# Two chained attention blocks on one core: the transpose that closes each pass of row maxima is put two jobs later

## The reference: what is computed

```
x = x + block0(groupnorm(x))    # per image: 1024 queries x 1024 keys, scores*0.25 + rel_h + rel_w, softmax, @v, projection
x = x + block1(groupnorm(x))    # per image: 7x7 neighbourhood + 16 register keys, mask, softmax, @v, projection
```

## The kernel before

| row job | stage | step | its phase starts at |
|---|---|---|---|
| L0 phase 2 | L0 | 19 | step 32 |
| L1 phase 0 | L0 | 31 | L1 main stage |
| L0 phase 3 | L0 | 44 | step 48 |
| L0 phase 4 | L0 | 60 | step 64 |
| L0 phase 5 | L0 | 76 | step 80 |
| L1 phase 1 | L0 | 93 | L1 main stage |
| L1 phase 2 | L1 | 24 | step 68 of L1 |
| L0 phase 0, next image | L1 | 60 | next L0 stage |
| L0 phase 1, next image | L1 | 98 | next L0 stage |

## Time and profile before

### The profile page before, as it was taken

How to read it: one execution, slowest core, us unless ns; L and a number is a source line. 1 busy time by engine, 2 the same in 40 slices (tenths; PEclk the granted TensorE clock), 3 DMA queues, 4 the chain that set the end, 5 groups by cost and what they waited for, 6 DMA issues and landing times.

```text
span 4900.8 us, 97559 instructions
## 1 busy us (share of the span) xinstructions
PE 4491.2 (92%) x32598; PEld 2291.5 (47%) x32598; DVE 3079.3 (63%) x5558; ACT 2608.5 (53%) x3955; POOL 892.5 (18%) x1901
## 2 busy tenths in 40 slices
PE   5879999999999999999999999999999999999998
PEld 3334453544535454453544535455454544535444
DVE  3736667665675656667566675656657566676654
ACT  1533556555564555556555564555646555565564
POOL 3112111222202212121212202212021121102111
PEclk7888999999999999999999999999999999999999
DMA  6334242443414433253433424433144432424401
GB/s 126 83 73 86 49 104 62 99 90 70 89 39 106 87 87 71 53 108 70 99 79 70 88 52 99 94 73 84 44 106 81 99 79 48 101 62 99 87 14 40
DMA packets 235869, 386.05 MB, mean 79 GB/s; under 512 B 58396, under 2 KB 133728, under 8 KB 235360
## 3 DMA queue, kind: packets, MB, share of 16 engines
q1 hardware_dynamic: 189280, 266.13, 23.8%
q10 hardware_dynamic: 21504, 75.51, 7.6%
q0 software_dynamic: 24576, 37.80, 4.8%
HBM read 227.79 MB, written 88.08 MB: 64 GB/s over the span
## 4 chain that ended last, share of the span: by engine, by line
PE 75%; DVE 9%; SPq 5%; issue 5%; DMA 5%; ACT 2%; DVEq 0%; ACTq 0%; POOL 0%
PE P L1135 15%; PE P L1153 14%; PE P L1094 13%; PE P L958 6%; PE P L959 6%; DVE mx L901 5%; PE P L1071 5%; PE P L1185 4%; PE P L1206 4%; PE P L1102 3%; DMA QA<-queries 2%; PE P L1178 1%; SPq L507 1%; DMA biases<-xn 1%; DVE mxc L907 1%
## 5 line engine op out<-in xcount | busy, mean ns | idle before, releaser
L901 DVE TENSOR_REDUCE mx<-P 128x1 f32<-128x512 f32 x3072 | 1923.2, 682 | 471.2 <-PE P L1094 467.9
L771 ACT ACTIVATE probs<-P 128x1024 f32<-128x1024 f32 x1536 | 1507.5, 1022 | 777.7 <-PE P L1153 777.0
L1094 PE MATMUL P<-K,AR 96*128 96x256 f16 x6144 | 1093.1, 282 | 42.9 <-DMA AR<-biases 26.7
L1153 PE MATMUL P<-AR,K 113*128 113x512 f16 x3072 | 924.8, 383 | 14.1 <-DMA AR<-mrow 13.6
L907 DVE TENSOR_REDUCE mxc<-P 128x1 f32<-128x336 f32 (+1 forms) x1536 | 648.2, 474 | 307.6 <-PE P L1103 304.0
L787 ACT ACTIVATE probs<-P 128x320 f32<-128x320 f32 (+3 forms) x1632 | 618.1, 436 | 405.2 <-PE P L1206 340.0
L1135 PE MATMUL P<-probs,V 128*17 128x512 f32 x6144 | 817.2, 604 | 9.9 <-ACT probs L771 9.9
L1094 PEld LDWEIGHTS P<-K,AR 96*128 96x128 f16 x6144 | 541.7, 99 | 566.9 <-DVE mx L901 198.3
L1153 PEld LDWEIGHTS P<-AR,K 113*128 113x128 f16 x3072 | 216.9, 98 | 676.6 <-ACT probs L771 517.8
L1206 PE MATMUL P<-A,K 113*128 113x320 f16 (+2 forms) x1536 | 447.1, 306 | 12.9 <-ACT probs L787 12.1
L1102 PE MATMUL P<-K,A 112*128 112x320 f16 (+1 forms) x1536 | 400.4, 295 | 53.4 <-DVE mx L901 35.8
(11 more groups left out here) (122 smaller groups left out, 3705.4 us busy)
## 6 DMA issues: line engine op xcount, KB each, us to landing
AR<-biases SPq DMA_DIRECT2D x384, 256.0 KB, 7.7
AR<-queries ACTq DMA_DIRECT2D x96, 512.0 KB, 5.8
biases<-xn SPq DMA_DIRECT2D x192, 256.0 KB, 2.9
AR<-queries ACTq DMA_DIRECT2D x96, 256.0 KB, 8.5
K<-oraw POOLq DMA_DIRECT2D x384, 64.0 KB, 4.8
xin<-in_x_dram SPq DMA_DIRECT2D x16, 768.0 KB, 10.5
queries<-oraw SPq DMA_DIRECT2D x384, 32.0 KB, 4.8
QA<-queries SPq DMA_DIRECT2D x192, 64.0 KB, 5.1
```

The source lines that it names most:

```text
L771: nc.scalar.activation(probs[:, u % RING, j:j + 2, :], P[:, b:b + 2, :], ACT.Exp).then_inc(p_done[0], 1)
L901: V_.reduce_max(mx[:, n // 2, n % 2:n % 2 + 1], bank, AX.X).then_inc(used, 1)
L1094: last = mm(bank[:, QD * (v % 2):QD * (v % 2) + QD], AR[0:ROWS_MAX[0], part % SLOTS, v, c, j, 128 * q:128 * q + 128], K0[0:ROWS_MAX[0], h, ...
L1153: last = mm(P[:, j, :], K0[0:ROWS, h, 128 * kt:128 * kt + 128], AR[0:ROWS, p % SLOTS, kt // 2, :, j, :], start=True, stop=True)
```

## The change

The list of placed jobs is sorted as before, and then `rows_later` goes through it from the end: each row job is taken out and put behind the next two jobs that are not DMA moves, as long as these stand at most two steps further on, are no row jobs themselves, and are not max jobs of L1 behind a row job of L1. Since those followers may be max jobs of the next phase, `mx` gets a second buffer (by the parity of the phase), and the row jobs get semaphores of their own, `row_done` and `row_used`, because the counts of `smax_done` and `smax_used` would otherwise no longer follow the order.

```diff
+def is_row(job):
+    return job[0] == "max" and job[4] == ITEMS[job[1]]
+
+def rows_later(placed):
+    for at in [n for n, (_, job) in enumerate(placed) if is_row(job)][::-1]:
+        to, passed = at, 0
+        while passed < 2 and to + 1 < len(placed):
+            follower = placed[to + 1][1]
+            if placed[to + 1][0] > placed[at][0] + 2 or is_row(follower) or follower[1] == 1 and placed[at][1][1] == 1 and follower[0] == "max":
+                break
+            to, passed = to + 1, passed + (follower[0] not in MOVES)
+        row = placed.pop(at)
+        placed.insert(to, (placed[to - 1][0] if to > at else row[0], row[1]))
+    return placed
...
-    for place, job in sorted(placed, key=lambda p: p[0]):
+    for place, job in rows_later(sorted(placed, key=lambda p: p[0])):
...
-        mx = sb("mx", [128, ITEMS[0] // 2, 2])
+        mx = sb("mx", [128, 2, ITEMS[0] // 2, 2])
...
-        smax_done = sems("smax_done")
-        smax_used = sems("smax_used")
+        smax_done, row_done = sems("smax_done"), sems("row_done")
+        smax_used, row_used = sems("smax_used"), sems("row_used")
...
+            if is_row(job):
+                return row_used[layer], image * PHASES[layer] + part + 1
+            return smax_used[layer], image * PER_ITEMS[layer] + part * ITEMS[layer] + n + 1
...
-                            V_.reduce_max(mx[:, n // 2, n % 2:n % 2 + 1], bank, AX.X).then_inc(used, 1)
+                            V_.reduce_max(mx[:, part % 2, n // 2, n % 2:n % 2 + 1], bank, AX.X).then_inc(used, 1)
...
-                                V_.tensor_reduce(mxc[0][:], mx[:], AX.X, ALU.max).then_inc(comb_done, 1)
+                                V_.tensor_reduce(mxc[0][:], mx[:, part % 2, :, :], AX.X, ALU.max).then_inc(comb_done, 1)
...
-                last.then_inc(smax_done[layer], 1)
+                last.then_inc((row_done if is_row(job) else smax_done)[layer], 1)
```

More of the change, by code:

```diff
@@ L333, in attention_kernel @@
         out_in = sem("out_in")
-        PER_ITEMS = [PHASES[n] * (ITEMS[n] + 1) for n in range(2)]
+        PER_ITEMS = [PHASES[n] * ITEMS[n] for n in range(2)]
         PER_Q, PER_K, PER_QA, PER_AR = 12 * 16, 12 * 16, 4 * 16, 6 * 16
@@ L382, in consumed @@
                 return stat_used[layer], image * 2 + n + 1
-            return smax_used[layer], image * PER_ITEMS[layer] + part * (ITEMS[layer] + 1) + n + 1
+            if is_row(job):
+                return row_used[layer], image * PHASES[layer] + part + 1
+            return smax_used[layer], image * PER_ITEMS[layer] + part * ITEMS[layer] + n + 1
         def rel_view(bank, n, operand):
@@ L893, in low_parts @@
                     if what == "max":
-                        dve.wait_ge(smax_done[layer], value)
+                        dve.wait_ge((row_done if is_row(job) else smax_done)[layer], value)
                         if n == ITEMS[layer]:
```

## The result

The changed kernel takes 4952.07 us (median of 4 runs, 4938.19 to 4958.52) against 4900.42 us for the kernel before on the same chip (4896.02 to 4903.14): ratio 1.011, 95% interval 1.0088 to 1.0132. It is slower, as forecast, but by some 52 us where 12 were forecast, and outside the range. The profiled execution is the fastest of the four, 4938.2 us with a span of 4936.4, so against the profiled execution of before (span 4900.8) it shows 36 of the 52.

A forecast was written before the change was run, and what follows sets the result against it. PE, busy 92% of the span, was taken to bound the kernel. Terms +10.4, +4, +4.0, -8.7, +4.2, -0.6 and -1.5 (job-only stage) sum to +11.8 us on the median 4898.6: 4910.4, range 4885 to 4930.

The forecast's parts named there:

- rival B: Late rows meet other traffic, ACT's large loads at phase 3: 1.2 us in 16 images, +19, 4930; chance 0.16.
- L1's phase 2: L1 steps 24 to 25: max job waits for its bank; +0.3 us an image, bounds 0 and 0.5, +4.2 in all.
- What bounds it: PE, busy 92%; row transposes' waits for DVE, 68.8 us, fall to 20 to 30, replaced by 30 to 47 DMA waits.
- Phase 3: L0 steps 44 to 48: SP issues the row's DMAs later, so scores wait; +0.65 us an image, +10.4 in all.
- Phase 4: L0 steps 60 to 64: transpose still waits for the combination, no gain; 0 an image, +4 us for late fourth DMAs.
- Phase 5: L0 steps 76 to 80: PE gains 0.7 but DMAs issue later; +0.27 us an image, +4.0 in all.
- L0's phase 0 in L1: L1 steps 60 to 62: scores and a max job fill the transpose's wait; -0.62 us an image, -8.7 in all.
- The two others: L0 phase 2 and L1 phase 0: almost no wait, DMAs have room; 0.03 and 0.01 us gained, -0.6 in all.
- Rival A: Rows land in time, so the waits go and nothing replaces them: -16 us, time 4882; chance 0.14.
- C: Losses are half of those counted, phase 3 at 0.4 and L1's phase 2 at 0: 4902, no change; chance 0.25.
- The 2.0 us per DMA: Skill's fixed DMA time against 1.7 measured; would add 0.3 on phases 3, 4 and 5, 14 us; measured value used.

The follow-up runs named there:

- the pair that differs in this row alone: Changed kernel moving only L1's rows, 1.0015, and one moving only the L0 phase 0 row inside L1, 0.9946, each against the kernel before.
- The pair 1.0111 and 1.0007: Changed kernel moving only L0's phase 3 row, 1.0111 against the kernel before; the same with the next phases' ACT and SP loads three steps later, 1.0007.
- L0's phase 0 alone: Changed kernel, buffer and semaphores included, moving only the L0 phase 0 row in L1's plan: 0.9946 against the kernel before.

## Why the prediction was wrong

The direction was right, and so were most of the steps. Two steps failed, and between them they hold most of what the sum missed.

The first is the overlap at phase 3. The sum lets the row's fourth DMA land after the usual 1.7 us, and leaves its meeting with ACT's load to rival B, at 1.2 us an image and a chance of 0.16. In its place the runs showed a landing of 3.8 to 6.7 us in 2 to 12 of 16 images, plus the first image's phase 1, for which the sum has no term. Without these hits the whole change costs 0.66% and not 1.10 or 1.68%. The second is the cost of L1's phase 2, +0.3 us an image. The wait behind it measured +0.64, and the pair that differs in this row alone puts the row at 0.7%, some 34 us, where 4.2 were counted.

- *What bounds it.* The transposes' wait was not worth its 68.8 us, as said: it fell to 30.2 (forecast 20 to 30), and 35 waits for the rows' DMAs came in (forecast 30 to 47).
- *Phase 3*, forecast +0.65 an image, measured +0.51 to +0.57 where the row was not hit. The two reductions in front of the negation took less: from the first max job to SP's first issue 2300.06 - 2298.14 = 1.92, where 2.01 were counted; the remaining path, 3.63, was 3.62. The kernels with phase 3 alone show the same in their undisturbed images.
- *Phase 4*, forecast 0 and +4 in all, measured +5.5. The transpose and its start were as said. What failed is the assumption that the fourth DMA is late only as often as before: in this trace the row took 0.6 to 1.0 us more than usual in 14 of 16 images. The four late rows before were read as chance, but an instruction fetch stands just behind this row, and the microsecond by which SP issues later puts the row into it. That the fetch is the cause rests on the 75 rows with it and the 121 without; no run moved it. The total came out near the forecast because two of the four late rows of before were worse than those of after, up to 0.97 us: in images 2 to 13 phase 4 costs 0.2 to 0.85 each, which is luck for the sum.
- *Phase 5*, forecast +0.27 an image, measured +0.11: in steps 75 to 78 the gain was 0.70, behind them the loss 0.81. SP issued 0.89 after the transpose started (2349.90 - 2349.01) where 1.10 were counted.
- *L0's phase 0 in L1*, forecast -0.62, measured -0.52 to -0.61, 8.1 us in all. The seven other traces that move this row show the same 8.1.
- *L1's phase 2*, forecast +0.3 with bounds 0 and 0.5, measured +0.64, constant from image to image. The wait was sized right, 0.4 for the bank, but the order behind the second `rel` job costs the max job 0.66 by its distance from DVE's addition, and none of it comes back. This part of the term was mis-sized by some 5 us over the run. The larger part has no place in the prediction at all: with this row moved the steps 0 to 25 ahead of it are longer too, by some 10 us in the traces, and why is open.
- *The two others*, forecast 0.03 and 0.01 gained an image, measured 0.25 gained in steps 16 to 32 and 0.31 lost in 32 to 43. Their sum is small because they cancel.
- *Rival B* is the first of the failed steps. The prediction named the mechanism and the time: the row's fourth DMA at 2276.56 against ACT's loads from 2276.36 on. Measured, ACT's load is 0.27 behind it, since it moved with V by the 0.35. It was priced at 1.2 us in each of 16 images, from the landing of 4.4 in the earlier trace rows. That one is the start-up row, which stands behind 1 MB of bias loads on its own queue and says nothing of this meeting. In truth it comes in 2, 5, 8 or 12 images, and then the landing is 2 to 5 us over the usual one, with up to 3.0 in the steps after it; and the first image pays it a second time, for its phase 1, with 6.3 us. The term was both mis-sized and given too small a chance (0.16). The pair 1.0111 and 1.0007 shows that it is nearly all the loss of that row.
- *Rival A* (waits go, nothing replaces them) fell with the 35 waits, *C* with its two terms: phase 3 lost 0.5 and not 0.4, and L1's phase 2 gave nothing back. The rival of the experiments, the semaphores and the buffer, fell as a cost with L0's phase 0 alone, which has both and is faster than before.
- The 2.0 us per DMA of the Trainium skill (DMA: Bandwidth & Descriptors, Anatomy of one DMA) was no help either way: the median landing stayed at 1.7.

Open: why the load's first packet starts 1.2, 1.3 or 1.4 us behind the row's fourth issue, at the same spacing of the issues, and so why the row is hit in 12 images of one kernel and 2 of another; why L0's steps 11 and 12 run at a clock of 0.52 less often in most kernels that move phase 0's row (0, 1, 2, 2, 5, 5, 6 and 7 of 15) than in the others (4, 6, 7, 9, 9 and 9); what lengthens L1's first steps when its phase 2 row moves; and whether a single DMA in place of four would have been immune, which was not tried.

## What to carry to other kernels

When a step is put later, follow it to its last DMA, and compare that one's issue with what every other queue issues in the next microsecond; a small transfer just ahead of a large one on another queue was a cliff here, and a cliff costs by chance, so price it at what one hit costs, with the clock after the wait, and by the share of hits from none to all. If one rule moves many places, price each place, then try the rule place by place: here two places of seven, L0's phase 3 and L1's phase 2, carried most of the loss, and the kernel with one other place alone has most of the gain. If a kernel's time scatters more than its predecessor's, look for such a cliff in it. And look at what moves just behind a transfer that is to come later: phase 4's row used to land just ahead of an instruction fetch, and a microsecond later it met it.

## What the runs showed of the hardware

- A DMA of 4 KB that lands in 1.7 us took 4.21 and 6.33 in the two cases shown, and 7.1 at the longest, when a load of 512 KB went out on the other queue 0.20 to 0.26 us behind it, and 1.7 when it was 1.37 behind. With four loads of 256 KB behind it on its own queue at 0.7 us it took the usual time.
- At the same distance of 0.25 to 0.26 us it was hit in some images and not in others, within one execution. It was hit when the load's first packet started 1.15 to 1.32 us after the small DMA's issue (31 rows), and not when it started at 1.38 or later (37 rows).
- After a wait of 4.7 us for such a DMA the granted clock was 0.64 over the next 5.6 us; after 5.4 us in the first image it was 0.50 over the next 3.6, the lower of PE's two levels.
- SP's four issues of phase 4's row took 2.8 to 3.5 us instead of 2.4 in 51 of 196 cases (images 2 to 15 of 14 traces), and in each of them a packet of instruction fetch started 1.06 to 1.94 us after the first issue.
